# Four graph layers on one core: leftover chunks re-read from stored gathers, ScalarE's exponentials two steps later, the sort's ranks after the gate products

## What is computed

```python
h_stack = jnp.einsum('ni,rdi->rnd', x, W)                 # 8 kinds of edges
h_src = h_stack[edge_type, src].reshape(-1, N_HEADS, HEAD_DIM)
h_dst = h_stack[edge_type, dst].reshape(-1, N_HEADS, HEAD_DIM)
attn_src = jnp.sum(h_src * a_src, axis=-1)
attn_dst = jnp.sum(h_dst * a_dst, axis=-1)
attn = jax.nn.leaky_relu(attn_src + attn_dst, negative_slope=0.2)
attn = jax.nn.softmax(attn, axis=0)                       # over all edges
msg = (h_src * attn[:, :, None]).reshape(-1, OUT_DIM)
out = jax.ops.segment_sum(msg, dst, num_segments=num_nodes)
```

## Time and profile before

| | us |
|---|---|
| median of 3 runs | 4981.04 (4974.59 to 4981.15) |
| the profiled execution | 4983.89 |
| its span, first to last instruction | 4982.0 |
| TensorE busy | 3979.3 (80%) |
| VectorE busy | 3409.0 (68%) |
| GpSimd busy | 3202.8 (64%) |
| ScalarE busy | 1799.4 (36%) |

### The profile page before, as it was taken

The page is one execution under the profiler, slowest core; times in us unless marked ns, Lnnn a source line. Parts: engine busy times, 40 slices in busy tenths (PEclk is TensorE's granted clock), DMA queues, the critical chain, the costliest instruction groups (busy, mean ns, idle before and its releaser), DMA issues. The chain is left out here.

```text
span 4982.0 us, 109658 instructions
## 1 busy us (share of the span) xinstructions
PE 3979.3 (80%) x22466; PEld 3275.0 (66%) x22467; DVE 3409.0 (68%) x9196; ACT 1799.4 (36%) x5526; POOL 3202.8 (64%) x3524
## 2 busy tenths in 40 slices
PE   6799996689987889878898466785967878578886
PEld 3477775677876778767787356674856667357665
DVE  7788886567756778577786667865237777755665
ACT  0454543121123333333332100012246667357774
POOL 0255554677756777667776677765677777247775
PEclk9799998899998999989999677897968888777787
DMA  1233333855525555264550787832454445234445
GB/s 45 91 120 120 117 120 98 196 143 153 161 61 172 147 145 159 58 191 136 149 160 21 229 246 218 243 101 82 144 101 107 102 102 105 57 97 108 108 109 99
DMA packets 633882, 637.83 MB, mean 128 GB/s; under 512 B 314926, under 2 KB 537460, under 8 KB 633716
## 3 DMA queue, kind: packets, MB, share of 16 engines
q0 software_dynamic: 149568, 384.54, 28.2%
q1 hardware_dynamic: 386164, 197.34, 14.6%
q10 hardware_dynamic: 97984, 54.35, 3.6%
HBM read 468.18 MB, written 166.84 MB: 127 GB/s over the span
## 5 line engine op out<-in xcount | busy, mean ns | idle before, releaser
L975 POOL DMA_INDIRECT G<-h_dram,idx x1572 | 1523.2, 969 | 534.8 <-issue 360.4
L1150 PEld LDWEIGHTS ps_a<-hotm,msg 128*128 128x128 f32 x4716 | 687.7, 194 | 202.1 <-DVE arena L1239 71.7
L1138 PE MATMUL ps_e<-nnw,attT 128*128 128x256 f32 x2358 | 736.1, 396 | 96.2 <-DVE prodm L1232 46.7
L1150 PE MATMUL ps_a<-hotm,msg 128*128 128x128 f32 x4716 | 729.4, 283 | 95.4 <-DVE arena L1239 93.0
L1239 DVE TENSOR_TENSOR arena<-ps_a,arena 128x256 f32 x1404 | 588.1, 419 | 214.3 <-issue 106.4
L770 POOL DMA_INDIRECT rec_dram<-rec,pos x392 | 378.7, 966 | 455.9 <-ACT rec L630 340.3
L975 POOL DMA_INDIRECT G<-feat_dram,idx x420 | 405.6, 966 | 266.9 <-POOLq L242 139.3
L1185 ACT ACTIVATE msg<-prodm 128x256 f32<-128x256 f32 x786 | 327.4, 417 | 669.4 <-DVE prodm L1232 597.0
L975 POOL DMA_INDIRECT arena<-rel_dram,idx x468 | 457.8, 978 | 158.4 <-issue 101.2
L792 POOL DMA_INDIRECT rec_dram<-now,to x396 | 391.2, 988 | 186.3 <-POOL to L789 103.4
L1138 PEld LDWEIGHTS ps_e<-nnw,attT 128*128 128x128 f32 x2358 | 368.2, 196 | 132.7 <-DVE prodm L1232 67.5
(11 more groups left out here) (349 smaller groups left out, 7953.2 us busy)
## 6 DMA issues: line engine op xcount, KB each, us to landing
gate<-rec_dram SPq DMA_DIRECT2D x126, 384.0 KB
G<-msg_dram SPq DMA_DIRECT2D x300, 128.0 KB
msg_dram<-msg ACTq DMA_DIRECT2D x270, 128.0 KB
rel_dram<-stage SPq DMA_DIRECT2D x25, 1040.0 KB
G<-h_dram,idx POOLq DMA_INDIRECT x1572
msg_dram<-arena ACTq DMA_DIRECT2D x90, 128.0 KB
at<-edge_attr SPq DMA_DIRECT2D x98, 112.0 KB
attT<-attT_dram SPq DMA_DIRECT2D x74, 144.0 KB
```

The costliest lines, as they stand in the source:

```text
L975: pool.indirect_dma_start(G[:, n % width, :], None, table, bass.IndirectOffsetOnAxis(ap=idx[:, which, n:n + 1], axis=0)).then_inc(sem(f"sw ...
L1138: t.matmul(ps_e[s % BANKS][:], attT[:, s // HU, s % HU, :], nnw[:], start=True, stop=True).then_inc(sem("ew"), 1)
L1150: last = t.matmul(ps_a[s % BANKS][:, h, :], of[:, h * P:(h + 1) * P], hot[:, s, :], start=True, stop=True)
```

## The change

Four things are changed.

1. In the sort's loop TensorE's first ranks (L677) stand behind the gate products instead of before them.
2. In the relational pass only the 393 main chunks are gathered. SyncE stores the first 75 gathered chunks, in which all leftovers lie, in `kept_dram`, and loads the window of each of the 75 extra units from there. The indices now take the leftover rows' true numbers (BIG is taken off), and a mask per chunk and row, added to the logits by a new VectorE instruction, gives rows that don't belong to the unit -1e30. SyncE's loads of `meta2` come six chunks earlier per part.
3. ScalarE's group exponentials go from lag 12 to lag 14, and it waits for additions once in four steps and for target logits once in two.
4. One turn of the scatter by source moves out of the block before the pass, through two blocks whose count stays the same, into the last block of the gated layer.

```diff
+    kept_d = dram("kept_dram", (KD * P, RW))
...
-                            if c0:
-                                n, i, s = c0
-                                b = s // 2
-                                if s % 2 == 0:
-                                    pe.wait_ge(sem("hot"), i * 2 + b + 1)
-                                    for j in range(SG - 1):
-                                        last = t.matmul(ps_r[:, j + 1:SG, :], identb[:], four(OK[:, b, j, :], SG - 1 - j),
-                                                        start=False, stop=(j == SG - 2), skip_group_check=True)
-                                    last.then_inc(sem("before"), 1)
                             if c2:
...
                             if c0:
-                                if s % 2 == 1:
+                                if s % 2 == 0:
+                                    pe.wait_ge(sem("hot"), i * 2 + b + 1)
+                                    for j in range(SG - 1):
+                                        last = t.matmul(ps_r[:, j + 1:SG, :], identb[:], four(OK[:, b, j, :], SG - 1 - j),
+                                                        start=False, stop=(j == SG - 2), skip_group_check=True)
+                                    last.then_inc(sem("before"), 1)
+                                else:
                                     pe.wait_ge(sem("looked_up"), i * 2 + b + 1)
...
-                            scatter_by_source(pool, (33, 39))
+                            scatter_by_source(pool, (33, 40))
...
-                            scatter_by_source(pool, (42, 44))
+                            scatter_by_source(pool, (43, 45))
...
-                            scatter_by_source(pool, (44, EC2 // (G2 * GROUPS2)))
+                            scatter_by_source(pool, (45, EC2 // (G2 * GROUPS2)))
...
-                            v.tensor_scalar(idx[:, 1, 0:SEAM * U], meta[:, 0:SEAM * U, 2], float(NOBODY), None, ALU.min)
+                            v.tensor_copy(idx[0:1, 0, 0:KD], starts)
+                            v.tensor_scalar(over, meta[:, :, 2], float(BIG), -float(BIG), ALU.is_ge, ALU.mult)
+                            step(v.tensor_scalar(valid, meta[:, :, 0], 0.0, None, ALU.is_ge))
+                            step(v.scalar_tensor_tensor(valid, meta[:, :, 0], float(P), valid, ALU.is_lt, ALU.mult))
+                            v.tensor_tensor(over, over, meta[:, :, 2], ALU.add)
+                            step(v.tensor_scalar(valid, valid, -NEG, NEG, ALU.mult, ALU.add))
+                            v.tensor_copy(idx[:, 1, 0:SEAM * U], over[:, 0:SEAM * U])
+                            v.tensor_copy(mask[:, 0:SEAM * U], valid[:, 0:SEAM * U])
...
-                            gather_rows(pool, (0, NU), rel_d, 1, G, "msg")
+                            for n in range(NC1):
+                                s = n % UR
+                                if n >= UR:
+                                    pool.wait_ge(sem("msg"), upto(n - UR))
+                                    if n - UR < KD:
+                                        pool.wait_ge(sem(f"g_out{s}"), n // UR * 16)
+                                pool.indirect_dma_start(G[:, s, :], None, rel_d, bass.IndirectOffsetOnAxis(
+                                    ap=idx[:, 1, n:n + 1], axis=0)).then_inc(sem(f"sw_g{s}"), 16)
...
+                            for n in range(KD):
+                                s = n % UR
+                                sp.wait_ge(sem(f"sw_g{s}"), gathered[s] + (n // UR + 1) * 16)
+                                sp.dma_start(kept_d[n * P:(n + 1) * P, :], G[:, s, :]).then_inc(sem(f"g_out{s}"), 16)
...
-                                sp.wait_ge(sem("msg"), upto(i * UR))
+                                sp.wait_ge(sem("msg"), upto(i * (UR - 6)))
...
+                            for s in range(UR):
+                                sp.wait_ge(sem(f"g_out{s}"), -(-(KD - s) // UR) * 16)
+                            for k in range(KD):
+                                if k % BACK == 0:
+                                    _, at = nc.values_load_multi_w_load_instructions(
...
+                                n = NC1 + k
+                                sp.wait_ge(sem("msg"), upto(n - UR))
+                                sp.dma_start(G[:, n % UR, :], kept_d[ds(at[k % BACK], P), :]).then_inc(sem(f"x_in{n % UR}"), 16)
...
-                            for c0, c1, c2, c5, c12, c28 in walk(nc.scalar, TURNSR, 0, 1, 2, 5, 12, 28, width=UR, static=TURNSR - LASTT):
+                            for c0, c1, c2, c5, c14, c28 in walk(nc.scalar, TURNSR, 0, 1, 2, 5, 14, 28, width=UR, static=TURNSR - LASTT):
...
-                                    act.wait_ge(sem("agg"), upto(n - UR))
+                                    if s % 4 == 0:
+                                        act.wait_ge(sem("agg"), upto(n + 3 - UR))
...
-                                    act.wait_ge(sem("ad_e"), upto(n - RING))
+                                    if s % 2 == 0:
+                                        act.wait_ge(sem("ad_e"), upto(n + 1 - RING))
...
-                                        act.wait_ge(sem(f"sw_g{j}"), gathered[j] + (i + 1) * 16)
+                                        if isinstance(i, int) and i * UR + j >= NC1:
+                                            act.wait_ge(sem(f"x_in{j}"), (i * UR + j - NC1) // UR * 16 + 16)
+                                        else:
+                                            act.wait_ge(sem(f"sw_g{j}"), gathered[j] + (i + 1) * 16)
...
                                     v.tensor_reduce(logit[:, q, :, :], picked[:, q, :, :, :], AX.X, ALU.add).then_inc(sem("summed"), 1)
+                                    dve.wait_ge(sem("summed"), upto(g))
+                                    v.tensor_tensor(logit[:, q, :, :], logit[:, q, :, :], mask[:, chunks].unsqueeze(2).to_broadcast([P, GR, NH]),
+                                                    ALU.add).then_inc(sem("masked"), 1)
...
-        normalize(turns=(39, 42), early=[(W_in, L2_gnn_W.rearrange("r (h p) d -> p r h d", p=P))])
+        normalize(turns=(40, 43), early=[(W_in, L2_gnn_W.rearrange("r (h p) d -> p r h d", p=P))])
```

More of the change, by code:

```diff
@@ L1527, in relational_attention @@
                 row = arena[:, row_at:row_at + NU]
+                mask_at = meta2_at + NC2 * REC2
+                mask = arena[:, mask_at:mask_at + NU]
                 with ExitStack() as pctx:
@@ L1618, in _ @@
-                            v.tensor_scalar(over, back[:, :, :, 2], -float(BIG + NOBODY), None, ALU.add)
-                            step(v.tensor_scalar(mask, back[:, :, :, 0], 0.0, None, ALU.is_ge))
-                            step(v.scalar_tensor_tensor(mask, back[:, :, :, 0], float(P), mask, ALU.is_lt, ALU.mult))
-                            step(v.tensor_tensor(over, over, mask, ALU.mult))
-                            v.tensor_scalar(idx[:, 1, NC1:NU].rearrange("p (t j) -> p t j", j=BACK), over, float(NOBODY), None, ALU.add)
+                            over, valid = LG[:, :, 0], LG[:, :, 1]
@@ L1623, in _ @@
+                            v.tensor_copy(mask[:, NC1:NU].rearrange("p (t j) -> p t j", j=BACK), late_valid[:, :, FRONT:U])
                             v.tensor_copy(row[:, 0:SEAM * U], meta[:, 0:SEAM * U, 0])
                             v.tensor_copy(row[:, SEAM * U:NC1].rearrange("p (t s) -> p t s", s=FRONT), front[:, :, :, 0])
-                            v.tensor_copy(mask, back[:, :, :, 0])
+                            v.tensor_copy(row[:, NC1:NU].rearrange("p (t j) -> p t j", j=BACK), back[:, :, :, 0])
@@ L1710, in _ @@
                             with nc.sync.Fori(0, GR) as i:
-                                sp.wait_ge(sem("msg"), upto(i * UR))
+                                sp.wait_ge(sem("msg"), upto(i * (UR - 6)))
                                 sp.dma_start(meta2[:, ds(i * PART, PART), :], rows[:, ds(i * PART, PART), :]).then_inc(sem("meta2_in"), 16)
+                            for s in range(UR):
[3 more added lines that the diff above has]
+                                    _, at = nc.values_load_multi_w_load_instructions(
+                                        idx[0:1, 0, k:k + BACK], engines=[mybir.EngineType.SP], min_val=0, max_val=(KD - 1) * P,
+                                        skip_runtime_bounds_check_because="starts are sums of the leftovers of the buckets before, under a chunk each")
+                                n = NC1 + k
+                                sp.wait_ge(sem("msg"), upto(n - UR))
+                                sp.dma_start(G[:, n % UR, :], kept_d[ds(at[k % BACK], P), :]).then_inc(sem(f"x_in{n % UR}"), 16)
                             sp.wait_ge(sem("meta2_in"), GR * 16)
@@ L1787, in _ @@
                             v = nc.vector
-                            credit(dve, "picked", "summed", "leaky", "most", "diag", "total", "high", "fall", "shifted",
```

(3 more changed lines are left out.)

14 lines of the change are left out of this document (7 added, 7 removed).

## The result

The changed kernel takes 4914.29 us (median of 4 runs, 4912.15 to 4917.72), the kernel before beside it 4979.51 (4974.59 to 4981.15): a ratio of 0.9872, 95% interval 0.986 to 0.9884, so 65 us or 1.3% faster. Forecast were 4917. The profiled execution took 4915.44 us, its span is 4913.3. It was run again later, on a chip where the kernel before took 4976.18: 4915.9, a ratio of 0.9874.

A forecast was written before the change was run, and what follows sets the result against it. The prediction held TensorE to bound the sort, and gathers and consumers to bind each other in the relational pass. Terms -28 - 9 - 13 + 4 - 25 + 2 + 5 = -64 us gave 4917 us, range 4900 to 4952.

The forecast's parts named there:

- sort: Sorting loop: ranks behind the gate products shorten a group from 6.65 to 6.32 us; -28 us taken.
- second semaphore: Relational pass: 75 gathers wait for a second semaphore, 0 to 0.15 us each; +4 us taken.
- mask: Relational pass: one more VectorE instruction per group, hidden under the gathers in 33 groups, open in six; +2 us.
- tail: Relational pass, gather 392 to last addition: consumers right behind the gathers need 103.7 us instead of 128.6; -25 us.
- scatter turn: Block before the pass: GpSimd ends last there, so one turn of six scatters fewer counts whole; -9 us.
- gathers without waits: Relational pass until gather 392: GpSimd becomes the bound and waits for nothing, 500 us instead of 513; -13 us.
- clears: Behind the pass: 73 more semaphores cleared at 0.07 us each while all engines stand; +5 us.
- rival B: Sorting loop: VectorE's chain, started by the moved ranks, holds the next group; -5 instead of -28, 4940 us; 14%.
- the bound of 500: Relational pass: GpSimd's gathering time without waits, 382.5 us busy plus 118 us of bare gaps.
- Rival A: Relational pass: waiting for gathers halves TensorE's clock, so consumers don't outrun the gathers; -35 us in all, 4946; 20%.
- Stores and loads: Relational pass: SyncE's 75 stores and 75 loads stay hidden behind the gathers; nothing, up to +5 us.

The follow-up runs named there:

- e1: Kernel before with only TensorE's first ranks moved behind the gate products, on a slower chip: 6167.5 us against 6211.11, ratio 0.9925.
- e0_after: The changed kernel itself, run again as a measure for its variants: 4915.9 us, ratio 0.9874 to the kernel before.
- e6: Changed kernel with ScalarE's exponentials back at lag 12, thinned waits kept: 4936.57 us, ratio 0.9913 to the kernel before.
- e3: Kernel before with only the stored chunks (stores, loads, mask, 393 gathers), run twice on slower chips: ratios 0.9973 and 0.9975.
- e2_scalar: Kernel before with only ScalarE's part (exponentials at lag 14, thinned waits), on a slower chip: 6190.51 us, ratio 0.996.

## Why the prediction was right, step by step

Forecast 4917, measured 4914.3; the sum was -64, the medians have -65.2 and the two traces -68.8. The mechanisms held, but that the sum came so near is in part luck: the sort and the second semaphore brought 6 and 4 us more than was taken, the mask 2; the tail and the gathers 6 and 2 us less. The rows below sum to -66.4; the other 2.4 us lie in blocks that the sum doesn't name.

| step | forecast | trace of after |
|---|---|---|
| sort | -28 | -33.8 |
| scatter turn | -9 | -8.8 |
| gathers without waits | -13 | -10.6 |
| second semaphore | +4 | 0, inside the row above |
| tail | -25 | -18.6 |
| mask | +2 | not seen, inside the rows above |
| clears | +5 | +5.4 |

**The sort: mechanism right, and I gave away part of it.** The steps were worked out as 3.08 and 3.24 us, a group as 6.32; they are 3.07, 3.25 and 6.32. 98 x 0.34 is 33. The prediction took -28 because "the idle row allows 29 at most". That ceiling was wrong. The row counts only the time in which no matmul ran; the weight load of the same ranks had stood 47.3 us for VectorE's rows in the waits of the kernel before, some of it beside running matmuls. A chain from transpose to transpose holds whatever of this counts, an idle row only what is bare; which of the two waits the other 4 us were in, no row says. VectorE's 0.6 us of slack held on chip I, and rival B got nothing; on chip II it was gone (e1).

**The scatter turn** came out as counted: from SyncE's last store to the first gather 6.4 us instead of 14.0. The turn that went to the gated layer cost nothing there: its last block ends 33.7 us sooner (3346.5 against 3380.2), which is the difference that the sort had made.

**The gathers.** The shape was right: GpSimd waits for nobody. The second semaphore was forecast at 0 to 0.15 us in 75 gathers, from a scatter whose gap was 0.59; the gap before gathers 37 to 111, which have the second wait, and before 112 to 393, which have not, is 0.305 us alike. Nor had the number of waits made the 0.59: in e1_ranks the same scatters have the same waits, and 88 of these 98 gaps are 0.30. What was short by 2 us was the bound of 500, from a bare gap of 0.30: 382.85 + 392 x 0.305 is 502.4, the stretch 502.3. By the same 0.305 GpSimd had waited 11 us before the change, and not 13 (85.3 + 45.5 less 393 x 0.305).

**The tail was mis-sized.** It was forecast as 103.7 us and is 109.5 (112.8 in e0_after): 6.4 us until the 94 last additions begin instead of 5.3; 66 of them at 1.13 us instead of 1.10; and the last 28 at 1.01 instead of 0.92, a pace taken from the last 24 additions, though the last 28 of the kernel before had taken 0.99 each.

**What made the consumers outrun the gathers** was said rightly, the three stands of 2.0 us in 36 chunks; e6 puts them back and loses 21 us. But the sum has no such row. It books the -25 of the tail under "393 gathers, exponentials later, fewer waits" as a whole, and a reader could have expected the stored chunks alone to bring most of it. On chip I they bring about nothing without the later exponentials (e6); and what the exponentials alone bring on chip I, without them, was not tried. The two belong together, as the prediction had said of easing both, and their 29 us can't be split between them.

**Rival A** failed on chip I, though its premise came true. ScalarE waits for gathers once per group (33 times, 87.8 us), and TensorE's granted clock falls behind such a wait. Windows of the additions in one group: stretch, length, additions, clock, DMA.

```profile
3813.60:3815.30 1.70, 0.84 (x2) 1.00 0.49 125
3815.30:3817.00 1.70, 0.00 (x0) 0.90 0.39 110
3817.00:3818.70 1.70, 0.11 (x1) 0.50 0.29 81
3818.70:3820.40 1.70, 0.74 (x2) 0.50 0.52 135
3820.40:3822.10 1.70, 0.43 (x2) 0.50 0.34 98
3822.10:3823.80 1.70, 0.42 (x1) 0.59 0.38 98
3823.80:3825.50 1.70, 0.42 (x1) 1.00 0.45 120
```

ScalarE's copy in this group stood 3.36 us for gathers (at 3816.2), no addition starts between 3814.8 and 3818.6, and the clock is 0.50 (1.2 GHz) from 3816.7 to 3823.5. It costs nothing, because the consumers have that time: over the gathers the clock is 0.87, up from 0.82, and the additions keep the gathers' pace (1.273 us, gathers 1.278). The Trainium skill ("TensorE: Matmul & The Clock Gate", HAM oscillation) describes this drop at each wait for DMA; the drop is in the trace, and what it makes of the time hangs on whether TensorE is the bound, which here it is not.

**Stores and loads** hid as forecast. The loads land in 2.1 us (median), the stores beside the gathers in 3.2. The Trainium skill ("DMA: Bandwidth & Descriptors", Anatomy of one DMA) had given an estimate of 2.3 for this size. It states that fit for DMAs issued by GpSimd, and these are SyncE's; the loads came near it, the stores did not.

## What to carry to other kernels

Where two loops hold each other through a ring, look at how far the consumers are behind, and why. If the distance is the whole ring because the consumers' own pace is slow (chip I, e6), taking work from the producer brings nothing until their stand is gone; if it is the way round the ring that is long (chip II, e3), it shortens the tail, here by 26 us of 162. In both cases the last lap of the ring is paid at the end. A result that comes 0.4 us late in each group cost nothing, as it didn't hold the engine that sets the pace; a second wait that was met cost GpSimd nothing. To size a reordering, take the time from one step's start to the next in the trace rather than the idle time of the engine, and add up a gain on one chip only: here the sort was worth 44 us on chip II and 34 on chip I, and the stored chunks 14 us by themselves on chip II and about nothing without the later exponentials on chip I.

## What the runs showed of the hardware

- One program took 4976 us on one chip and 6211 and 6209 us on two others, with VectorE's, ScalarE's and GpSimd's instructions of equal length: the time was between them. ScalarE, where it waited, took up TensorE's product 0.13 us (median) behind its end on the first and 1.2 us (e2_scalar) on another; from the first gather to the first addition went 57 us instead of 34.
- A second semaphore wait before GpSimd's gather, when it is met, adds nothing: a gap of 0.305 us with one and with two.
- A clear of a semaphore at a barrier costs about 0.07 us (101 in 7.4, 35 in 2.4), as forecast: 5.4 us for 73 new ones.
